# Self-attention unit of a two-layer cross-attention kernel: both peak matmuls of a step are issued behind its score matmuls

## The reference

```
def attention(x, ctx, wq, wk, wv, wo, bo):
    q = x @ wq
    k = ctx @ wk
    v = ctx @ wv
    ...                                     # 16 heads of 64
    sim = jnp.einsum('bhid,bhjd->bhij', q.astype(jnp.float32), k.astype(jnp.float32)) * scale
    attn = jax.nn.softmax(sim, axis=-1).astype(v.dtype)
    out = jnp.einsum('bhij,bhjd->bhid', attn, v)
    out = out.transpose(0, 2, 1, 3).reshape(b, n, HEADS * D_HEAD)
    return out @ wo + bo
...
x = x + attention(layer_norm(x, g1, b1), layer_norm(x, g1, b1), wq1, wk1, wv1, wo1, bo1)
```

## Time and profile before

| | us |
|---|---|
| median of 3 runs | 2436.41 (2434.92 to 2436.89) |
| the profiled execution, its own time | 2436.33 |
| its span in the profile | 2434.6 |
| TensorE busy over the span | 2183.5 (90%) |
| VectorE busy | 1747.9 (72%) |
| ScalarE busy | 1477.4 (61%) |
| GpSimd busy | 1158.5 (48%) |

### The profile page before, as it was taken

The page is one execution under the profiler, slowest core; times in us unless marked ns, Lnnn a source line. Parts: engine busy times, 40 slices in busy tenths (PEclk is TensorE's granted clock), DMA queues, the critical chain, the costliest instruction groups (busy, mean ns, idle before and its releaser), DMA issues.

```text
span 2434.6 us, 59106 instructions
## 1 busy us (share of the span) xinstructions
PE 2183.5 (90%) x25392; PEld 1447.4 (59%) x25392; DVE 1747.9 (72%) x3148; ACT 1477.4 (61%) x1948; POOL 1158.5 (48%) x730
## 2 busy tenths in 40 slices
PE   4999998899799999899959999989996999998998
PEld 1566665675356666567525666656753666666675
DVE  6888886555588888565558888865556888885664
ACT  2788787234288888633328888772333787885342
POOL 4667656122176675522217676552222666654231
PEclk8999999999799999999969999999998999999999
DMA  3222220000131231000023223100001212210000
GB/s 85 68 69 51 76 60 26 1 19 16 33 88 50 58 88 41 25 8 12 16 68 81 57 58 82 47 25 1 19 16 46 75 49 70 76 35 19 10 10 18
DMA packets 52437, 106.62 MB, mean 44 GB/s; under 512 B 9552, under 2 KB 13648, under 8 KB 52176
## 3 DMA queue, kind: packets, MB, share of 16 engines
q1 hardware_dynamic: 52176, 102.84, 15.9%
HBM read 50.25 MB, written 2.10 MB: 21 GB/s over the span
## 4 chain that ended last, share of the span: by engine, by line
PE 63%; DVE 19%; ACT 9%; issue 4%; DMA 2%; POOL 1%; SPq 1%; POOLq 0%; DVEq 0%; ACTq 0%
PE scores L689 7%; PE scores L691 7%; PE scores L690 7%; PE work L770 7%; PE scores L797 6%; PE scores L790 6%; DVE minima L1306 6%; DVE prob L1321 4%; PE work L689 3%; PE work L690 3%; PE work L691 3%; ACT prob L1123 3%; PE work L819 3%; PE work L815 3%; PE work L817 3%
## 5 line engine op out<-in xcount | busy, mean ns | idle before, releaser
L637 POOL TENSOR_TENSOR prob<-prob 128x1024 f16<-128x1024 f32 x256 | 582.7, 2276 | 554.2 <-ACT prob L1124 543.4
L1306 DVE TENSOR_REDUCE minima<-work 128x1 f32<-128x512 f32 x1024 | 681.5, 683 | 52.4 <-PE work L770 36.4
L1123 ACT ACTIVATE prob<-scores 128x1024 f32<-128x1024 f32 x512 | 526.0, 1027 | 125.2 <-PE scores L797 108.2
L1124 ACT ACTIVATE prob<-scores 128x1024 f16<-128x1024 f32 x512 | 523.0, 1021 | 0.0
L815 PE MATMUL work<-vals,prob 128*128 128x65 f16 x4096 | 430.1, 193 | 15.5 <-POOL prob L637 13.3
L819 PE MATMUL work<-vals,prob 128*128 128x65 f16 x4096 | 430.6, 196 | 0.0
L817 PE MATMUL work<-vals,prob 128*128 128x64 f16 x4096 | 430.5, 193 | 0.0
L815 PEld LDWEIGHTS work<-vals,prob 128*128 128x128 f16 x4096 | 383.8, 99 | 77.7 <-POOL prob L637 14.9
L770 PE MATMUL work<-ka,qa 128*128 128x512 f16 x1024 | 402.0, 396 | 25.3 <-DMA kb<-staged_k 16.1
L817 PEld LDWEIGHTS work<-vals,prob 128*128 128x128 f16 x4096 | 380.7, 97 | 58.1
L819 PEld LDWEIGHTS work<-vals,prob 128*128 128x128 f16 x4096 | 381.2, 97 | 0.0
(11 more groups left out here) (166 smaller groups left out, 4469.8 us busy)
## 6 DMA issues: line engine op xcount, KB each, us to landing
qa<-staged_q SPq DMA_DIRECT2D x128, 128.0 KB, 2.4
ka<-staged_k SPq DMA_DIRECT2D x128, 128.0 KB, 2.4
raw_even<-in_pairs SPq DMA_DIRECT2D x32, 384.0 KB, 3.4
raw_odd<-in_pairs SPq DMA_DIRECT2D x32, 384.0 KB, 3.3
raw_odd<-in_pieces SPq DMA_DIRECT2D x20, 512.0 KB, 3.6
raw_even<-in_pieces SPq DMA_DIRECT2D x20, 512.0 KB, 3.7
qb<-staged_q SPq DMA_DIRECT2D x64, 128.0 KB, 2.4
kb<-staged_k SPq DMA_DIRECT2D x64, 128.0 KB, 2.4
```

Of the source, the lines that this page charges most:

```text
L637: pool.tensor_tensor(prob[1][:, slot, :], prob32[:, slot, :], prob[0][:, slot, :], ALU.subtract).then_inc(a.polished, 1)
L1123: act.activation(prob32[:, n % RING, :], source, ACT.Exp)
L1124: act.activation(prob[0][:, n % RING, :], source, ACT.Exp)\
L1306: dve.tensor_reduce(minima[:, t, h:h + 1], out[:, :], AX.X, ALU.max, negate=True)\
```

## The change

Each step's two peak matmuls stood apart: the first ahead of the placed product and the scores, the second behind the scores. Now both stand behind the scores and behind the `take`. The `arrive` step, a wait for the next pair's q and k in step 7 of head 1, moves with the first of them. No step is added or removed.

```diff
     for s in range(TILES):
         peaks = [step for step in peaks_of[s] if step.kind == "max"]
         if s == TILES - 1 and after:
             out.append(Step("shift", 0, *nxt, 0))
-        out += [step for step in peaks_of[s] if step.kind == "arrive"] + peaks[:1]
         out += placed[s]
         out.append(Step("score", s, par, head, 0))
         out += [take(step) for step in placed[s] if step.kind in HIGH]
-        out += peaks[1:] + [step for step in peaks_of[s] if step.kind == "combine"]
+        out += [step for step in peaks_of[s] if step.kind == "arrive"] + peaks + [step for step in peaks_of[s] if step.kind == "combine"]
         out += loads[s]
         if s >= 1:
             out += low(s - 1, par, head)
```

## The result

| | before | after |
|---|---|---|
| median | 2436.39 us (2434.92 to 2436.89) | 2476.94 us (2475.55 to 2478.94) |
| span of the profiled execution | 2434.6 us | 2475.3 us |
| TensorE busy | 2183.5 us (90%) | 2186.8 us (88%) |
| GpSimd busy | 1158.5 us | 1241.4 us |

The changed kernel takes 1.0176 of the time before (95% interval 1.016 to 1.0192), 40.6 us more. The forecast was 2485 us, in the range 2456 to 2506. It was right in direction and mechanism and 8 us too high.

A forecast was written before the change was run, and what follows sets the result against it. The prediction took PE's transpose waiting for DVE's combine as the bound. Head 0 units 12.2, head 1 units with merges 32.4 and the first pair's head 1 units 3.6 made 48 us on 2436.3, so 2484.5 us, range 2456 to 2506.

The forecast's parts named there:

- The loop closed at the transpose: PE's transpose waits for DVE's combine in every unit; whatever delays the combine lengthens the unit by the same amount.
- Step 5's reduce, +0.60: Step 5's first reduce, formerly done while DVE waited for ACT's copy, now stands behind the take: +0.60 us.
- The peak matmul, -0.22: The peak matmul leaves the step's front, so scores, exponentials and copies come 0.22 us earlier from the transpose.
- The race in step 3 of head 1: POOL's subtraction now starts 0.47 us before DVE's refine, which must wait; the combine is 1.35 us late in all.
- The refine of step 7 unaffected: In head 1, step 7's refine was already held to POOL's subtraction's end, so the 0.38 us shift is hidden.
- rival C: Head 0 step 3: POOL's subtraction, 0.07 us behind, overtakes the refine; +18 us, 2503 us; chance 0.13.
- rival D: Head 0 step 5: the refine, 0.16 us ahead, falls behind POOL's polish; 58 us more, 2542 us; chance 0.04.
- B: Only the shift's delay: head 1's flip does not happen or DVE absorbs it; +23 us, 2459 us; chance 0.18.
- E: Hidden anyway: the combine is not what PE really waits for; 2436 us; chance 0.05.
- F: Faster: scores come one matmul earlier, the reduce is hidden; each unit gains 0.22, 2423 us; chance 0.04.
- The row's transfer at 0: The shift row's transfer has one matmul less to hide behind before the next unit; 0 taken, bound 7 us.
- rival A: The forecast itself, head 0 and head 1 losses together: 2484.5 us, own range 2474 to 2494; chance 0.56.

The follow-up runs named there:

- e4: The kernel before with the first peak moved behind scores and take in step 5 alone: 2469.38 us, ratio 1.0136.
- e5: The kernel before with the first peak moved in step 3 of head 1 alone: 2475.69 us, ratio 1.0152.
- e11: The changed kernel with POOL's subtraction of the split in step 3 of head 1 made to wait for that step's refine: 2459.42 us.
- v3: The kernel before with both peaks leading in step 5 of head 0 and step 6 of head 1, the combine directly behind the second: 2419.97 us.
- e9: The changed kernel with step 3 of head 1 alone put back as it was: 2468.42 us, ratio 1.0126.
- e1: The changed kernel with POOL's 768-column split of head 1 moved from step 3 to step 4: 2488.5 us, ratio 1.0231.

## Why the prediction was right, point by point

- *The loop closed at the transpose.* Shown. Unit lengths follow the combine's lateness in every kernel; in the changed kernel's pair the combine came 23.40 us after the previous transpose instead of 22.14, and the unit grew by 1.26. In the unit read from each of the twelve kernels the transpose follows the combine's start by 0.30 to 0.32 us.
- *Step 5's reduce, +0.60.* Shown by e4: both heads lost 0.60.
- *The peak matmul, -0.22.* Right in sign, uneven in size. In head 0 the take of `ck` came 0.16 us earlier (18.99 instead of 19.15 after the transpose). In head 1 step 3's scores came 0.31 earlier than in a steady unit before (11.34 instead of 11.65), and the control unit's take of `cv` 0.30 earlier (17.56 instead of 17.86). Net of the reduce that makes +0.44 in head 0 and +0.30 in the control unit, where the forecast had 0.38 for both. e4 showed what the forecast did not say: the credit only exists if the scores of the step ahead have moved too.
- *The race in step 3 of head 1.* Shown by e5 and e11, and by the control unit. POOL's lead was 0.48 us, forecast 0.47; the refine took 2.25, where the prediction's list of signs says 2.4 and its own times (324.22 to 326.40) give 2.2 to 2.3. The unit before that the rows show is 0.06 us longer than a steady one, and everything read from it is 0.06 later, so the steady unit is the better measure: the merge's take came at 16.15 us after the transpose instead of 15.43, 0.72 late, forecast 0.82; the `cv` product 0.71, forecast 0.82; its take 0.72 (18.58 instead of 17.86), forecast 0.75; with the reduce the combine was 1.32 late (23.40 instead of 22.08), forecast 1.35. Part of the closeness is luck. PE's chain gained 0.31 and not 0.22 ahead of the race, and ACT's copy followed PE by 0.20 and not by 0.13. These two misses nearly cancel. That the path runs through the merge's take is borne out by the first pair, which has no merge: there the refine of step 3 also took 2.25 us, but the take of `cv` came at 17.35 instead of 17.43, and the unit lost only 0.50.
- *The refine of step 7 unaffected.* Its end was; its length fell from 1.98 to 1.60 as it started later behind the same subtraction. In v3 it became the point where a gain was lost.
- *Near ties that held.* Head 0's step 3 (rival C) kept its order: the refine led by 0.06 us, forecast 0.07. Step 5 (rival D) kept it with 0.17, forecast 0.16. Rivals B, E and F are out.
- *The row's transfer at 0.* PE's wait for it was 4.2 us against 3.8.
- *A slip in rival A's own range.* With the second term halved (-16.2) or a third larger (+10.8) the sum is 2468 to 2495, and 2502 with the transfer's 7 us, not 2474 to 2494. The measured time lies in either range.
- *Waits ahead of the takes.* The forecast said that they grow by a reduce each. For `ck` they grew from 15.0 to 21.6 us only, and for `cv` they fell from 23.2 to 20.3: in the changed kernel the reduces of step 4 stand behind their take too and fill the gap (steady head 1 unit: 0.56 us before and after).

The terms of the sum that were mis-sized:

| term | forecast | measured |
|---|---|---|
| head 0 units | 32 x 0.38 = 12.2 | 20 x 0.44 = 8.8, four of the second pair at 0.1 and four of the last at 0.3 on average: 10.4 |
| head 1 units with merge | 24 x 1.35 = 32.4 | 23 x 1.32 + 0.30 = 30.7 |
| head 1 of the first pair | 4 x 0.9 = 3.6 | 4 x 0.50 (21.38 to 21.88) = 2.0 |

That is 43 us against 48; the median moved by 40.6. The forecast counted as steady 12 head 0 units that are not. Those of the second pair had been longer than the steady ones before, 23.50 us. The refine of step 7 at their start, with POOL 0.15 us ahead, took 2.58 us, where the steady ones took 1.98; that this is the cause is not shown. After, they are as long as the others (23.60). Why the last pair's lost less stays open; its four values spread from -0.09 to +0.85 us. The first unit of each round varies by 2 to 3 us between the kernels and can't be read. The forecast also overlooked the one unit without a split.

## What to carry to other kernels

Find the instruction at which a software-pipelined loop closes, follow it back to the last wait for another engine, and count what stands behind that wait: it costs in full. Work ahead of it is free only if what ends the wait does not hang on it. Step 5's first reduce was such work before; step 3's refine was not, since the copy of `cv` hangs on it by way of the merge's take and PE. Where two engines exclude each other, treat each pair of near starts as a race with a margin, and check each margin against every shift that an edit makes, since a move of 0.6 us on one engine can cost a whole instruction of the other; here a semaphore that fixes the order (2459.42 us) was cheaper than restoring the order by the schedule (e9, 2468.42) or putting the split off (e1, 2488.5). And a matmul into a short ring of banks belongs ahead of other work only where the reduce that frees its bank is surely done.

## What the runs showed of the hardware

The order of the two starts decides who loses, and the start of the first decides when the second ends. With POOL's 768-column subtraction ahead by 0.14, 0.48, 0.74 and 1.13 us, DVE's refine took 2.58 (v3), 2.25 (changed), 1.98 and 1.60 us (changed, step 7 at 296.62) instead of 1.22. Lead and length add up to 2.72 us within 0.02 each time, in every such refine of the twelve traces. Behind a 1024-column subtraction the sum is 3.21 (0.75 ahead, 2.47 long, in e1). So a narrow defeat costs most, up to 1.36 us here, and with the refine ahead by as little as 0.06 us it costs DVE nothing: the refine keeps its 1.22. POOL's side is alike: a polish that starts 0.17 to 1.05 us behind a refine that itself ran free ends about 3.2 us after the refine's start, whatever its own start. The Trainium skill's page SBUF — State Buffer, section "Who interferes with whom", says that the port pair that VectorE and GpSimd share is an exclusive lock and that the issue order decides who blocks; these runs agree with it down to 0.06 us. DVE's reduces from PSUM and the takes beside them kept their 0.60 us spacing beside POOL's instructions in the head 1 stretches shown.
